# Head of an int8 stage: maxima of pairs, a first group tile by tile, spread latent products

## What is computed

```python
outlier = jnp.any(jnp.abs(xf) > THRESHOLD, axis=0)
x_int = jnp.where(outlier[None, :], 0.0, xf)
x_out = jnp.where(outlier[None, :], xf, 0.0)
row_absmax = jnp.maximum(jnp.max(jnp.abs(x_int), axis=1), 1e-08)
Cx = jnp.round(x_int * (127.0 / row_absmax)[:, None]).astype(jnp.int8)
acc = jnp.matmul(Cx.astype(jnp.int32), CB.T.astype(jnp.int32))
out_i8 = acc.astype(jnp.float32) * (row_absmax[:, None] / 127.0) * (SCB[None, :] / 127.0)
W_deq_T = CB.T.astype(jnp.float32) * (SCB / 127.0)[None, :]
out = out_i8 + jnp.matmul(x_out, W_deq_T) + bias[None, :]
...
x = x + out
```

## Time and profile before

| | us |
|---|---|
| median of 3 runs | 1683.25 |
| lowest, highest | 1673.1, 1688.26 |
| the profiled execution, its own time | 1679.22 |
| its span, first to last instruction | 1677.5 |

### The profile page before, as it was taken

How to read it: one execution, slowest core, us unless ns; L and a number is a source line. 1 busy time by engine, 2 the same in 40 slices (tenths; PEclk the granted TensorE clock), 3 DMA queues, 4 the chain that set the end, 5 groups by cost and what they waited for, 6 DMA issues and landing times.

```text
span 1677.5 us, 20601 instructions
## 1 busy us (share of the span) xinstructions
PE 1583.9 (94%) x7752; PEld 1289.1 (77%) x7752; DVE 833.7 (50%) x1318; ACT 506.1 (30%) x761; POOL 312.6 (19%) x262
## 2 busy tenths in 40 slices
PE   7898777999999879998999999999999999999996
PEld 5787546988987558886888888887878888888875
DVE  4666368986475545773333333333733333333336
ACT  4443223343336541223222222212242222222112
POOL 1000011134326550021311101112012111111110
PEclk9999898999999999999999999999999999999998
DMA  8765423556675667795271111112924411111115
GB/s 303 215 191 165 131 75 114 179 177 222 201 246 163 248 216 262 274 377 172 84 141 41 48 50 50 50 51 75 360 93 103 98 50 50 50 50 50 51 38 175
DMA packets 117240, 238.56 MB, mean 142 GB/s; under 512 B 22503, under 2 KB 61551, under 8 KB 115778
## 3 DMA queue, kind: packets, MB, share of 16 engines
q1 hardware_dynamic: 82042, 155.27, 27.8%
q0 software_dynamic: 23008, 68.24, 13.7%
q10 hardware_dynamic: 12112, 14.00, 2.8%
HBM read 164.51 MB, written 89.19 MB: 151 GB/s over the span
## 4 chain that ended last, share of the span: by engine, by line
PE 76%; DVE 5%; POOL 2%; issue 2%; DMA 2%; ACT 1%; SPq 0%; ACTq 0%; DVEq 0%; POOLq 0%
PE pu L1924 26%; PE pd L1924 25%; PE l_po L1924 6%; PE pf L1924 6%; POOL scratch_pairs L1433 2%; PE pw L640 2%; PE pw L639 2%; PE l_ea L1286 2%; PE l_ea L1857 1%; PE l_po L1857 1%; PE pg L1066 1%; PE l_tr L1872 1%; DMA delta<-scratch_expert_out 1%; PE l_ea L1872 1%; DVE y1T L942 1%
## 5 line engine op out<-in xcount | busy, mean ns | idle before, releaser
L1924 PE MATMUL pd<-down_hi,hid_hi 128*128 128x512 f32 x640 | 249.2, 389 | 2.9 <-issue 2.9
L1924 PE MATMUL pu<-y_hi,up_hi 128*128 128x512 f32 x640 | 249.3, 389 | 0.0
L1924 PE MATMUL pu<-y_lo,up_hi 128*128 128x512 f32 x640 | 249.1, 389 | 0.0
L1924 PE MATMUL pd<-down_hi,hid_lo 128*128 128x512 f32 x640 | 249.0, 389 | 0.0
L1924 PE MATMUL pd<-down_lo,hid_hi 128*128 128x512 f32 x640 | 249.0, 389 | 0.0
L1924 PE MATMUL pu<-y_hi,up_lo 128*128 128x512 f32 x640 | 249.0, 389 | 0.0
L2225 DVE TENSOR_TENSOR hid_lo<-hidden,hid_hi 128x512 fp32r<-128x512 f32 x64 | 44.3, 692 | 388.2 <-ACT hid_hi L2133 388.2
L2055 POOL TENSOR_TENSOR down_lo<-raw,down_hi 128x1024 fp32r<-128x1024 f32 x40 | 100.3, 2508 | 678.4 <-ACT down_hi L2070 678.4
L2127 ACT ACTIVATE hidden<-pu 128x512 f32<-128x512 f32 x64 | 38.3, 598 | 467.6 <-PE pu L1924 467.6
L2164 DVE TENSOR_TENSOR acc<-pd,acc 128x512 f32<-128x512 f32 x224 | 143.6, 685 | 54.8 <-PE pd L1924 51.5
L1924 PEld LDWEIGHTS pd<-down_hi,hid_hi 128*128 128x128 f32 x640 | 120.2, 188 | 28.6 <-issue 3.7
(11 more groups left out here) (317 smaller groups left out, 2508.7 us busy)
## 6 DMA issues: line engine op xcount, KB each, us to landing
X<-scratch_x SPq DMA_DIRECT2D x256, 64.0 KB, 2.5
l_x<-scratch_x SPq DMA_DIRECT2D x32, 512.0 KB, 6.3
delta<-scratch_expert_out SPq DMA_DIRECT2D x32, 512.0 KB, 6.9
raw<-in_up SPq DMA_DIRECT2D x32, 512.0 KB, 3.7
raw<-in_down SPq DMA_DIRECT2D x32, 512.0 KB, 4.5
y1T<-in_x SPq DMA_DIRECT2D x16, 512.0 KB, 9.6
scratch_x<-y1T SPq DMA_DIRECT2D x16, 512.0 KB, 3.2
scratch_x<-l_x SPq DMA_DIRECT2D x16, 512.0 KB, 5.6
```

The lines of the kernel that those rows point to most:

```text
L1924: mm = pe.matmul(out, lhs[a], rhs[b], start=first and n == 0, stop=last and n == len(pairs) - 1)
```

## The change

1. **Maxima of pairs.** `row_peaks` is no longer one TENSOR_REDUCE over four blocks, but two TENSOR_TENSORs: the maximum of blocks 0-1 with 2-3, in place in `row_mag`, then of the two that are left, into `row_peak`. `peaked` counts 5 a group instead of 3 (`PEAKS`).
2. **First group tile by tile.** `scale` and `round_` go over tile 0, then `low(0)`, then tile 1. `round_` takes a first tile and a count; for tiles 0 and 1 it is 8 instructions each. Both halves of group 0's magnitudes have room of their own and follow each other.
3. **Second tile's parts in another place.** `z` of tile 1 is `z_one`, not in the latents' memory; `high(1)` and `low(1)` stand ahead of the loop. `x2` slots are swapped, so `add(0, ..)` needs no latents and `add(1, ..)` needs 24 units.
4. **Group 1 earlier.** `magnitudes(1, 0)` and `row_peaks(1, 0)` stand ahead of the loop.
5. **Bias additions later.** POOL waits for `z_lo` 1 ahead of the first.
6. **Latents spread.** 16 units ahead of `product(0, 0)`, then 3 + 5 after `product(0, 1)` (around `broadcast(1)`), 4 after `product(1, 1)`, 4 after `product(2, 0)`. `latent_out` follows them. The load of `l_war` on ACT's queue goes behind the first magnitudes.

```diff
+    z = [buf["z_one"] if t == 1 else buf["z"][t % 2] for t in range(NT)]
...
-            sp.dma_start(tile_of(SC["x2"], t), x2[:, t % 2, :]).then_inc(x2_stored[t % 2], 16)
+            sp.dma_start(tile_of(SC["x2"], t), x2[:, (t + 1) % 2, :]).then_inc(x2_stored[t % 2], 16)
...
     def gpsimd(pool):
         ahead["tables"](pool)
         pool.wait_ge(bias_loaded, 16)
+        pool.wait_ge(z_lo, 1)
...
-        ahead["war"](act)
         act.wait_ge(kept, 2)
         magnitudes(0, 0)
+        magnitudes(0, 1)
+        ahead["war"](act)
         latent_out(0)
+        magnitudes(1, 0)
         latent_out(1)
-        magnitudes(0, 1)
         latent_out(2)
+        high(0)
+        high(1)
         latent_out(3)
...
-            dve.tensor_reduce(peak[:, i, 0:n, :].unsqueeze(3), mag[:, 0:n, :, :].rearrange("k t p j -> k t j p"), AX.X,
-                              ALU.max).then_inc(peaked, 1)
+            dve.tensor_tensor(half[:, :, 0:2, :], half[:, :, 0:2, :], half[:, :, 2:4, :], ALU.max).then_inc(peaked, 1)
+            dve.wait_ge(peaked, at + 1)
+            dve.tensor_tensor(peak[:, i, 0:n, :], half[:, :, 0, :], half[:, :, 1, :], ALU.max).then_inc(peaked, 1)
...
-        latent(0, 13)
+        latent(0, 6)
         turn(0)
-        latent(13, 18)
+        latent(6, 10)
         broadcast(0)
-        latent(18, 32)
+        latent(10, 16)
...
                 product(s, 0)
+            if s == 2:
+                latent(28, 32)
...
                 product(s, 1)
+            if s == 0:
+                latent(16, 19)
+                broadcast(1)
+                latent(19, 24)
+            if s == 1:
+                latent(24, 28)
```

More of the change, by code:

```diff
@@ L729, in phase_l1 @@
     base_hi, base_lo = K["l2_base"]
-    x1, x2, bias, z, y2, stage, mag, peak, row, tmp, pf, pv, pt, pb, pg = [buf[n] for n in (
-        "x1 x2 bias z y2 stage mag peak row tmp pf pv pt pb pg").split()]
+    x1, x2, bias, y2, stage, mag, peak, row, tmp, pf, pv, pt, pb, pg = [buf[n] for n in (
+        "x1 x2 bias y2 stage mag peak row tmp pf pv pt pb pg").split()]
+    z = [buf["z_one"] if t == 1 else buf["z"][t % 2] for t in range(NT)]
     gout, g_stored = K["g_out"], K["g_stored"]
@@ L743, in phase_l1 @@
     LATE = 8
+    PEAKS = 5
     group_of = [g for g, (t0, n) in enumerate(GROUPED) for _ in range(n)]
-    first = {t0: g for g, (t0, n) in enumerate(GROUPED)}
+    whole = [KC * t + KC if t < GROUPED[0][1] else KC * (GROUPED[0][1] + group_of[t]) for t in range(NT)]
     def store_y2(sp, t):
@@ L854, in latent_out @@
                           gout[:, n % 2, :].rearrange("p (c j) -> p c j", c=NLAT)).then_inc(g_stored[n % 2], 16)
-        ahead["war"](act)
         act.wait_ge(kept, 2)
         magnitudes(0, 0)
+        magnitudes(0, 1)
+        ahead["war"](act)
         latent_out(0)
+        magnitudes(1, 0)
         latent_out(1)
-        magnitudes(0, 1)
         latent_out(2)
+        high(0)
+        high(1)
         latent_out(3)
-        latent_out(4)
-        high(0)
-        latent_out(5)
         for s in range(NT):
-            if s == 0:
+            if s == 1:
+                latent_out(4)
+                latent_out(5)
+            if s == 2:
                 latent_out(6)
-                latent_out(7)
             g, n, j = None, 0, 0
@@ L876, in scalar @@
                     g = group_of[s] + 1
-            if g and j == 0:
+            if g and j == 0 and s:
                 magnitudes(g, 0)
@@ L885, in scalar @@
                 magnitudes(g, 1)
-            if s + 1 < NT:
+            if s == 2:
+                latent_out(7)
+            if 1 <= s < NT - 1:
                 high(s + 1)
@@ L935, in scale, with round_ @@
                                   pb[:, j * P:(j + 1) * P].unsqueeze(1).to_broadcast([P, KC, P]), ALU.mult).then_inc(scaled, 1)
-        def round_(g, p0, p1):
-            t0, n = GROUPED[g]
+        def round_(t0, n):
             dve.wait_ge(scaled, t0 + n)
-            for p in range(p0, p1):
+            for p in range(KC):
                 part = y[:, t0:t0 + n, p, :]
@@ L947, in low @@
                 dve.wait_ge(f_mm, 2 * (t - 1))
-            dve.wait_ge(rounded, KC * (group_of[t] + 1))
-            dve.tensor_tensor(z[t % 2][1][:], y[:, t, :, :], z[t % 2][0][:].bitcast(F32), ALU.subtract).then_inc(z_lo, 1)
+            dve.wait_ge(rounded, whole[t])
+            dve.tensor_tensor(z[t][1][:], y[:, t, :, :], z[t][0][:].bitcast(F32), ALU.subtract).then_inc(z_lo, 1)
         def add(t, h):
@@ L959, in add @@
             dve.wait_ge(f_mm, 2 * t + h + 1)
-            dve.scalar_tensor_tensor(out=x2[:, t % 2, half], in0=pf[h][:], scalar=row[:, t:t + 1], in1=K["scb_row"][:, half],
+            dve.scalar_tensor_tensor(out=x2[:, (t + 1) % 2, half], in0=pf[h][:], scalar=row[:, t:t + 1], in1=K["scb_row"][:, half],
                                      op0=ALU.mult, op1=ALU.mult).then_inc(x2_part, 1)
             dve.wait_ge(x2_part, 2 * t + h + 1)
-            dve.tensor_tensor(x2[:, t % 2, half], x2[:, t % 2, half], x1[:, t % 2, half], ALU.add).then_inc(x2_made, 1)
+            dve.tensor_tensor(x2[:, (t + 1) % 2, half], x2[:, (t + 1) % 2, half], x1[:, t % 2, half], ALU.add).then_inc(x2_made, 1)
         dve.tensor_reduce(cmax[:].unsqueeze(2), K["top"][:].rearrange("p t k -> p k t"), AX.X, ALU.max).then_inc(kept, 1)
@@ L973, in vector @@
         quotients(0)
-        scale(0, 0, 4)
-        round_(0, 0, KC)
+        scale(0, 0, 1)
+        round_(0, 1)
+        scale(0, 1, 2)
         low(0)
+        round_(1, 1)
+        row_peaks(1, 0)
+        low(1)
         for s in range(NT):
@@ L1051, in product @@
             for k in range(KC):
-                last = split_product(pe, pf[h][:], [v[:, k, :] for v in z[t % 2]],
+                last = split_product(pe, pf[h][:], [v[:, k, :] for v in z[t]],
                                      [K["cbT"][:, k, h * HALF:(h + 1) * HALF]], k == 0, k == KC - 1)
@@ L1101, in tensor @@
                 turn(g)
-            if g and ((n == 2 and j == 0) or (n == 4 and j == 1)):
+            if g and n == 4 and j == 1:
                 broadcast(g)
@@ L2382, in build @@
         phase_first(nc, K, A, SC)
+        z_one = [place(nc, UPPER, f"z_one_{part}", 194496 + 4 * D * i, [P, KC, P], F32R) for i, part in enumerate(("hi", "lo"))]
         with ExitStack() as both:
```

38 lines of the change are left out of this document (20 added, 18 removed).

## The result

| | before | after |
|---|---|---|
| median of 20 runs each, us | 1680.95 | 1664.75 |
| lowest to highest | 1673.1 to 1688.26 | 1660.51 to 1674.92 |
| ratio, 95% interval | | 0.9908 [0.9893, 0.9923] |
| span of the profiled execution | 1677.5 | 1665.2 |

The ratio times 1680.95 is a gain of 15.5 us, with an interval of 12.9 to 18.0. The predicted time was 1668, the predicted gain 13.5.

What follows compares the result with a forecast made beforehand. PE sets the pace from 290 us on, VectorE in the head before; head steps bring tile 4's first product from 291.17 to 277.6, 13.5 us: 1679.2 - 13.5 = 1665.7, or 1669.8 from the median; taken 1668, range 1655 to 1680.

Steps and rivals of the forecast that it cites:

- turn(0) and the quotients: Group 0 in the head: turn(0) at 206.2 us instead of 213.08, quotients done at 210.4.
- Tile 0: Scale, eight narrow roundings (1.6 us), high and low part: product(0, 0) at 216.4 us, after 0.4 us of PE idle.
- The collision: POOL's bias additions from 219.9 us hold VectorE's group 1 work: turn(1) at 227.4 us instead of 224.5.
- The bias wait moves nothing: POOL's new wait for z_lo 1 is over at 216.4 us, before the additions start at 219.9.
- First and second stall: PE idles 7.1 us ahead of turn(1) (7.98 before), then 0.5 instead of 6.51 ahead of product(2, 0), at 252.0.
- Third stall: Around turn(2), a bias addition blocks group 2's peaks: PE idles 0.5 and 0.6 us (3.32 and 0.58 before).
- The clock drop that I kept here: Around turn(2), two short waits still bring the low clock, as before, so no difference is counted.
- add(3, 0): Ends at 271.1 us, just ahead of a bias addition; if caught, tile 4 comes 2.4 us late, gain 11.
- The wait at 369 stays: PE's wait at 369 to 370 us starts with a turn that PE sets, so it stays.
- rival 2: The stall at 369 goes too: 3.3 us more, gain 16.8, 1665 us or below; depends on POOL's phase; chance 0.12.
- Sum: Head gain of 13.5 us at tile 4's first product: 1665.7 us from the profiled execution, 1669.8 from the median.
- The forecast of no change: Whole kernel: time within 1% (16.8 us), the limit of what a measurement can tell; chance 0.67.

Runs made afterwards that it cites:

- e8: Changed kernel without POOL's new wait for z_lo 1 ahead of the bias additions; tile 4's first product at 76.9 us (changed kernel 79.1).
- e1: Changed kernel with POOL's bias additions waiting for all row peaks of group 1; turn(1) at 27.4 us instead of 30.1, tile 4's first product at 76.3.
- e2: Changed kernel with one reduction for row peaks again instead of pairs of maxima; turn(1) at 28.8 us, tile 4's first product at 80.7.
- e4: Changed kernel with latent units 16 to 23 moved between product(0, 0) and turn(1); tile 4's first product at 75.8 us, ratio to the kernel before 0.9877.
- e12: Second run of the changed kernel without POOL's wait for z_lo 1; tile 4's first product at 79.1 us.
- e9: Changed kernel with POOL's second base_lo waiting until group 4's quotients are made; tile 4's first product at 78.2 us, rest 1381.7 us.
- e11: The changed kernel run again, unedited; tile 4's first product at 78.4 us (79.1 in the first profile).
- e5: e4 with POOL's second, third and fifth bias additions waiting for later VectorE steps; tile 4's first product at 69.8 us, ratio to the kernel before 0.9853.
- e10: e5 and e9 together; tile 4's first product at 69.9 us, ratio to the kernel before 0.9862, 1655.6 us against 1678.8 beside it.
- e3: Changed kernel with all 32 latent units ahead of product(0, 0) again; tile 4's first product at 83.1 us.
- e6: Kernel before with the maxima of pairs alone; turn(1) at 42.3 us instead of 45.4, tile 4's first product at 88.5 instead of 92.9.
- e7: Changed kernel with ScalarE's high(0) ahead of the third latent_out; tile 4's first product at 78.4 us, rest 1390.9 us.

## Why the prediction was right, point by point

- **turn(0) and the quotients**: expected 7.96 us after the start (206.2), came at 7.7; the row maxima's chain took what it took before. Right.
- **Tile 0**: `product(0, 0)` 18.2 expected, 19.2 measured. Two terms were small, and one of them cost time. Eight roundings of 128 took 2.14 us, not 1.6, inside the bounds of 1.4 to 3.2: 0.34 each and 0.26 from start to start. That was hidden by a gap of 0.4 us that I had put between them and the high part: in e8, where nothing else holds the high part, it follows at once and `product(0, 0)` is at 18.3. The Trainium skill's rule of a fixed cost for small instructions ("VectorE: DVE Perf Modes", in the section on the TRN2 errata) points the right way, and its 1.0 us for eight is half of the 2.14 measured. The term that cost the 1.0 us is the store, which landed 1 us later in this execution and between 0.6 before and 0.5 after the expected time in others; whether `l_war`'s later load has a part in it was not tested.
- **The collision**: turn(1) expected at 29.2, measured 30.1, and 29.2 to 30.3 in other executions. It held other instructions than I had worked out (the first L919 and low(1), not the maxima of the second half), for the same sum: 10.9 us from product(0, 0) to turn(1), 11.0 expected. e1 shows the cause and its size, 8.4 for this step where I had 8.1. The Trainium skill's port rule ("SBUF — State Buffer", "SBUF: two separate sides") agrees with these rows, and e2 with its other half: the reductions, with one input, took 2.93 and 2.78 us beside the additions. But the prediction says it of two inputs alone and then counts group 0's roundings as an example, which have one tensor input and a column of scalars. They are held as well (2.43 instead of 0.40; eight of 384 in 5.73 instead of 3.67 in e4), and so are tiny ones of 4 columns (1.83 and 2.24 us). The Trainium skill's rule names, beside two inputs, instructions in a 2-port mode; that the roundings run in one no run here shows.
- **The bias wait moves nothing**: right, POOL began 2.2 us after z_lo 1, when x1 had landed, and e8 with e12 show no effect.
- **First and second stall**: 6.94 for 7.1, and 0.53 for 0.5. Tile 2's product at 55.4 against 53.8 expected, the 1.6 us being the 1.0 of tile 0 and the clock's longer low stretch (0.7 us more for product(0, 1)).
- **Third stall**: the maximum was held, 2.64 us, as expected. The clock drop that I kept here did not come (clock 1.00 from 255.08 to 278.79), and PE waited 0.54 instead of 0.5 and 0.6: here the sum was 1.9 too high. Tile 4 at 79.1 against 79.4: that it fits to 0.3 us is luck, 1.6 too little ahead of tile 2 and 1.9 too much behind it.
- **add(3, 0)** had its second instruction running (272.92 to 273.61, its usual 0.69 us) when the addition began at 273.13; the addition waited and took 2.75 us instead of 2.38. It began 0.2 us ahead of being caught. e4 shows the price when it is caught: 2.79 us, and 2.54 of wait.
- **The wait at 369 stays**: right, for a reason that was only half there. I had it begin with a `turn` that PE sets; e9 shows that behind the same `turn` PE doesn't wait once POOL is out of the way, so it depends on POOL, as rival 2 had it, and POOL holds the same two instructions before and after the change. The 1.9 us of clock in rival 2's price come and go from one execution to the next (e11).
- **Sum**: 13.8 us in the traces, 15.5 [12.9, 18.0] in the ratio. That is 0.92%, within the 1% that I called a measurement's limit. The forecast of no change by that bound held by little: 1% lies inside the interval of the gain. The 1668 was chosen between two sums, 1665.7 and 1669.8, by which time of before they start from; that the measured 1664.75 lies 1 us from the first is luck as well.

## What to carry to other kernels

In these runs a VectorE instruction with two SBUF inputs, and also a TENSOR_SCALAR from SBUF to SBUF, was held while a GpSimd addition or subtraction ran, and a reduction was not. So count a reduction replaced by two maxima as a gain where no GpSimd instruction can fall on it, and look for the DMA that starts that instruction. A semaphore meant to move work later does nothing when a load behind another semaphore is later still; the way to place it is to wait for the end of the instructions that must not be held (e5, e9). Work that fills a stall has to stand directly ahead of the waiting instruction: eight units placed one product too late left 6.9 us open (e4). And before a drop or a wait is put down to an edit, run the unchanged kernel again: e11 took the clock out of e9's account.

## What the hardware showed that I had not expected

Which waits of PE bring the low clock is not told by their length. Waits of 2.54 and 3.03 us (e4), 3.32 (before) and 6.94 (after) did, and so did 1.17 and 0.58 us around turn(2) in e2; 1.70 us did not in the kernel after, nor did 2.12 us in e5 and e10, which ran the head at the full level from 5.5 us after the stage's start on. The table by stretch of e10, behind that wait of 2.12:

```profile
242.40:246.40 4.00, 3.93 (x17) 1.00 0.54 184
```

The two short waits at group 4's quotients (0.71 to 1.36 us, then 0.61) were followed by the low level in before, after, e1, e3 and e6, and by the full one in e2, e4, e5, e7, e8, e11 and e12, and the longest of them, 1.36 in e8, is among the latter. The kernel after and e11 are one program. What decides there is open. And what the low level behind the wait ahead of turn(1) cost differed by up to 1.4 us between executions of one order, which with one late store makes up the 2 us of scatter at tile 4.
